# A branch prefetch hint at the head of every register loop of a graph, attention and expert layer

## What is computed

```python
edge_index = jnp.stack([src, dst])
xn = _layernorm(x, axis=-1)
x = x + _L0_gnn_ref(xn, edge_index, W, b) + _L0_mix_ref(xn[None], Wq, bq, Wk, bk, Wv, bv, Wo, bo, orf)[0]
x = x + _L0_ffn_ref(_layernorm(x, axis=-1)[None], gate_w, gate_b, expert_w, expert_b)[0]
```

## Time and profile before

| what | value |
|---|---|
| median of 3 runs | 1639.91 us (1638.55 to 1640.23) |
| the profiled execution | 1637.92 us, of which the span of the records is 1636.1 us |
| mean granted TensorE clock | 0.965 |
| PE busy | 1487.4 us (91% of the span) |
| DVE, ACT, POOL busy | 745.7, 436.5, 340.1 us |
| edge iterations on PE | 89, in 10 loops (534 matmuls of L1357, six each) |
| loop ends on PE | 127 records of COMPARE_BRANCH: 89 at L1352, 7 at L380, 5 at L1542, 23 at L1622, 3 at L386 |

### The profile page before, as it was taken

The page is one execution under the profiler, slowest core; times in us unless marked ns, Lnnn a source line. Parts: engine busy times, 40 slices in busy tenths (PEclk is TensorE's granted clock), DMA queues, the critical chain, the costliest instruction groups (busy, mean ns, idle before and its releaser), DMA issues.

```text
span 1636.1 us, 25212 instructions
## 1 busy us (share of the span) xinstructions
PE 1487.4 (91%) x8053; PEld 1215.6 (74%) x8054; DVE 745.7 (46%) x1414; ACT 436.5 (27%) x727; POOL 340.1 (21%) x332
## 2 busy tenths in 40 slices
PE   5888899999989999999999999997999589999980
PEld 2556666644459999999999999996888478888870
DVE  7855553220014545454545454534454425544535
ACT  6401121210003333333333333333122113322310
POOL 7403131112201010101011111001324222111133
PEclk9999999999999999999999999998999589999995
DMA  4100011412112020202020202003243425666657
GB/s 148 49 4 23 4 32 36 152 58 90 65 48 91 14 90 13 90 13 90 13 90 13 90 13 90 0 1 93 76 139 104 169 78 209 239 240 234 212 187 285
DMA packets 55022, 150.64 MB, mean 92 GB/s; under 512 B 7178, under 2 KB 14298, under 8 KB 54528
## 3 DMA queue, kind: packets, MB, share of 16 engines
q1 hardware_dynamic: 48288, 127.20, 21.8%
q0 software_dynamic: 6688, 22.83, 4.4%
HBM read 119.72 MB, written 48.64 MB: 103 GB/s over the span
## 4 chain that ended last, share of the span: by engine, by line
PE 87%; DVE 4%; issue 3%; DMA 2%; POOL 2%; ACT 1%; DVEq 1%; POOLq 0%; SPq 0%; ACTq 0%
PE PB L1407 11%; PE PB L1436 7%; PE PB L1438 7%; PE PB L1437 7%; PE PB L1357 6%; PE PB L1612 5%; PE PB L1613 5%; PE PB L1615 5%; PE PB L1472 4%; PE PB L1495 4%; PE PB L1395 2%; PE PB L1418 2%; PE PB L1396 2%; PE PB L1397 2%; PE PB L1420 2%
## 5 line engine op out<-in xcount | busy, mean ns | idle before, releaser
L1436 PE MATMUL PB<-xh,hw 128*128 128x416 f32 (+1 forms) x576 | 206.2, 358 | 4.9 <-POOL orfl L686 4.9
L1438 PE MATMUL PB<-xh,hw 128*128 128x416 f32 (+1 forms) x576 | 204.2, 355 | 0.0
L1437 PE MATMUL PB<-xl,hw 128*128 128x416 f32 (+1 forms) x576 | 204.1, 354 | 0.0
L1407 PE MATMUL PB<-h,AT 128*128 128x512 f32 x400 | 171.9, 593 | 1.2 <-ACT h L829 1.2
L1612 PE MATMUL PB<-mwh,mth 128*128 128x512 f32 x368 | 149.0, 405 | 1.3 <-issue 1.3
L1357 PE MATMUL PB<-ohs,ohd 128*128 x534 | 118.7, 347 | 32.2 <-issue 26.1
L1407 PEld LDWEIGHTS PB<-h,AT 128*128 128x128 f32 x400 | 76.1, 190 | 96.4 <-issue 94.4
L1613 PE MATMUL PB<-mwl,mth 128*128 128x512 f32 x368 | 144.6, 393 | 0.0
L652 POOL CAST hw<-hraw 128x1024 fp32r<-128x1024 f32 x24 | 24.9, 1037 | 477.5 <-PE PB L1438 469.1
L1357 PEld LDWEIGHTS PB<-ohs,ohd 128*128 x534 | 51.1, 96 | 97.3 <-issue 80.0
L867 ACT ACTIVATE qf<-PB,biasT 128x416 f32<-128x416 f32 (+1 forms) x48 | 29.2, 609 | 321.9 <-PE PB L1438 321.9
(11 more groups left out here) (234 smaller groups left out, 2862.4 us busy)
## 6 DMA issues: line engine op xcount, KB each, us to landing
mraw<-expert_w SPq DMA_DIRECT2D x64, 512.0 KB, 7.5
slot_y<-x SPq DMA_DIRECT2D x7, 2560.0 KB, 11.7
slot_y<-ybuf SPq DMA_DIRECT2D x46, 256.0 KB, 3.3
xrow<-x SPq DMA_DIRECT2D x20, 256.0 KB, 2.8
y_scratch<-xrow SPq DMA_DIRECT2D x20, 256.0 KB, 2.0
yrow<-y_scratch SPq DMA_DIRECT2D x20, 256.0 KB, 2.9
x2n_half<-xhat SPq DMA_DIRECT2D x20, 256.0 KB, 2.5
out<-x SPq DMA_DIRECT2D x9, 512.0 KB
```

Of the source, the lines that this page charges most:

```text
L1407: ins = mm(bank(4 + u % 2), AT[:, b, t * P:(t + 1) * P], hh[c][:, b, :], start=(b == 0), stop=(b == TT - 1))
L1436: mm(bank(i, n), hw[:, wi, 0, k, :], xh[:, k, c0:c0 + n], start=(k == 0), stop=False)
L1437: mm(bank(i, n), hw[:, wi, 0, k, :], xl[:, k, c0:c0 + n], start=False, stop=False)
L1438: ins = mm(bank(i, n), hw[:, wi, 1, k, :], xh[:, k, c0:c0 + n], start=False, stop=(k == KT - 1))
```

## The change

Each register loop is now written with `nc.Fori(..., engines=OrderedEngineSet([eng.engine]), hint_back_edge=True)` instead of `eng.Fori(...)`. The loop itself is the same, and so are its bounds. [...] It is done for all loops of all engines: 17 hints stand in PE's code, 17 in DVE's, 7 in ACT's, 2 in POOL's and 8 in SP's. Line numbers grow by one, for an import.

```diff
+from concourse.bass import OrderedEngineSet
...
         def pairs(eng, pair):
 
-            with eng.Fori(0, KT - 1) as j:
+            with nc.Fori(0, KT - 1, engines=OrderedEngineSet([eng.engine]), hint_back_edge=True) as j:
...
         def experts(eng, expert):
 
-            with eng.Fori(0, E // 2 - 1) as e2:
+            with nc.Fori(0, E // 2 - 1, engines=OrderedEngineSet([eng.engine]), hint_back_edge=True) as e2:
...
                 begin = dve.value_load(rngi[0:1, 3, b:b + 1], min_val=0, max_val=PAIRS * TT)
-                with dve.Fori(0, count) as i:
+                with nc.Fori(0, count, engines=OrderedEngineSet([dve.engine]), hint_back_edge=True) as i:
...
                 mm(PB[:, 1536 * s + P * b:1536 * s + P * b + P], eye[:, :], eye[:, :], start=False, stop=False, skip_group_check=True)
-                with pe.Fori(0, count) as i:
+                with nc.Fori(0, count, engines=OrderedEngineSet([pe.engine]), hint_back_edge=True) as i:
...
-            with pe.Fori(0, TT // 2) as g:
+            with nc.Fori(0, TT // 2, engines=OrderedEngineSet([pe.engine]), hint_back_edge=True) as g:
...
                 more, begin = tiles(pe, e)
-                with pe.Fori(0, more + 1) as i:
+                with nc.Fori(0, more + 1, engines=OrderedEngineSet([pe.engine]), hint_back_edge=True) as i:
```

More of the change, by code:

```diff
@@ L431, in load_weights @@
                     sp.dma_start(raw[:, i, :], w[i // KT, i % KT]).then_inc(r.raw[i], 16)
-                with sp.Fori(1, r.chunks * KT // 4) as g:
+                with nc.Fori(1, r.chunks * KT // 4, engines=OrderedEngineSet([sp.engine]), hint_back_edge=True) as g:
                     for i in range(4):
@@ L475, in _ @@
             sp.dma_start(qf[:, 0:M], orf).then_inc(a_orf, 16)
-            with sp.Fori(1, KT) as j:
+            with nc.Fori(1, KT, engines=OrderedEngineSet([sp.engine]), hint_back_edge=True) as j:
                 for i, w in enumerate((wk, wv, wq)):
@@ L489, in _ @@
             load_weights(ro, wo)
-            with sp.Fori(1, TT // 2) as g:
+            with nc.Fori(1, TT // 2, engines=OrderedEngineSet([sp.engine]), hint_back_edge=True) as g:
                 for i in range(2):
@@ L547, in expert @@
                 more, begin = tiles(sp, e)
-                with sp.Fori(0, more) as i:
+                with nc.Fori(0, more, engines=OrderedEngineSet([sp.engine]), hint_back_edge=True) as i:
                     store_tile(tile_of(begin + i), e, last)
@@ L686, in _ @@
             g.tensor_tensor(orfl[:, :], qf[:, 0:M], orfh[:, :].bitcast(F32), ALU.subtract).then_inc(a_cst, 1)
-            with pool.Fori(0, KT - 1) as j:
+            with nc.Fori(0, KT - 1, engines=OrderedEngineSet([pool.engine]), hint_back_edge=True) as j:
                 for i in range(3):
@@ L746, in _ @@
             more, begin = tiles(pool, E - 1)
-            with pool.Fori(0, begin + more + 1) as T:
+            with nc.Fori(0, begin + more + 1, engines=OrderedEngineSet([pool.engine]), hint_back_edge=True) as T:
                 gather_tile(tile_of(T + 1))
@@ L842, in high_pass @@
             def high_pass(r, src, c):
-                with act.Fori(0, TT // 2 - 1) as g:
+                with nc.Fori(0, TT // 2 - 1, engines=OrderedEngineSet([act.engine]), hint_back_edge=True) as g:
                     for p in range(2):
@@ L959, in expert @@
                 more, begin = tiles(act, e)
-                with act.Fori(0, more) as i:
+                with nc.Fori(0, more, engines=OrderedEngineSet([act.engine]), hint_back_edge=True) as i:
                     for h in range(2):
@@ L1075, in row_pass @@
             def row_pass(r, src, finish, c):
-                with dve.Fori(0, TT // 2 - 1) as g:
+                with nc.Fori(0, TT // 2 - 1, engines=OrderedEngineSet([dve.engine]), hint_back_edge=True) as g:
                     for p in range(2):
@@ L1284, in expert @@
                 more, begin = tiles(dve, e)
-                with dve.Fori(0, more) as i:
+                with nc.Fori(0, more, engines=OrderedEngineSet([dve.engine]), hint_back_edge=True) as i:
                     for h in range(2):
```

## The result

| | before | after |
|---|---|---|
| median of 4 runs | 1639.63 us (1638.55 to 1640.23) | 1648.74 us (1646.94 to 1650.44) |
| the profiled execution | 1637.92 us, span 1636.1 | 1646.94 us, span 1645.2 |
| mean granted TensorE clock | 0.965 | 0.967 |

The ratio is 1.0056, 95% interval 1.0039 to 1.0074: the changed kernel is 9.1 us slower. The forecast was 1650, which is 1.3 us from the median.

What follows compares the result with a forecast made beforehand. PE's sequencer was taken to bound the edge loops: 89 hints at 0.11 us add 9.8 us, all others 0, giving 1647.7 for the profiled execution and, with the median 2.0 above, 1649.7 (1650); 8-in-10 range 1640 to 1662.

Steps and rivals of the forecast that it cites:

- the 3.3 us of the experts' tiles: In the experts' tile loop, PE's sequencer was said to run 3.3 us ahead of its array, so hints add 0.

Runs made afterwards that it cites:

- four-buffer kernel: Kernel before with edge loops of 512 edges an iteration, one-hot buffers at constant addresses, 49 iterations instead of 89, no hint: 1615.83 us, ratio 0.9859.

## What to carry to other kernels

In a short register loop, ask first which ends last, the sequencer, the array or the producer of the operands: here, where the profile showed "issue" between full groups of matmuls while the producer waited for PE, each sequencer instruction cost 0.09 to 0.16 us an iteration, whatever it did, and the gain lies in taking some away (constant buffer addresses, fewer waits, more work in an iteration), which here was worth 24 us, until DVE became the bound. The hint saved time only on the sequencer whose body was fetched again (2.0 us a return on SP, with six packets of code an iteration), and cost 8.7 us in PE's edge loop, where 12 packets of code in the 263 us from 12 to 275 leave no fetch for most of its 79 returns; so look at the packets of the instruction queues inside the loop first. A lead is to be read at the loop's worst entry, not at one of its steady passes: the 3.3 us of the experts' tiles were about half used at the start of an expert.

## What the runs showed of the hardware

- With a hint at the head of PE's edge loop the branch at its end took 225 to 228 ns (median) instead of 207 to 215, with 46 packets of code before and after the change.
- One MOVE with an increment has a slot of 131 ns on PE's sequencer, an EVENT_SEMAPHORE 151 to 159, the hint 89, an ALU_OP 60 to 103, with records of 31, 51, 31 and 32 to 36 ns: the length of a record tells little of the price.
- A body of some 540 instructions on SP costs its sequencer 2.4 to 2.5 us at each return, 0.40 to 0.45 with the hint. A body of about 1,050 on PE came round with a branch of 208 ns (median), 0.06 us to the next record and no packet.
- Holes of PE can be put down to DVE although DVE is not waited for (14 in the changed kernel). The slot of the waiting instruction, 97 ns against 103 before, told that. In the four-buffer kernel the waits are real, and its weight loads start 0.05 us behind the one-hot's end.
